# One weight load for two moving blocks in narrow expert bodies, an earlier branch, and a later first wo remainder

## The reference

```python
logits = tokens @ gate_weight.T            # tokens: layer-normed x, 2048 x 512; 8 experts
probs, top1 = softmax(logits), argmax(logits)
mask = one_hot(top1) * (rank_within_expert < 320)   # capacity 320
hmid = gelu(dispatch @ wi)                 # per expert: (<=320) x 512 @ 512 x 2048
eout = hmid @ wo                           # (<=320) x 2048 @ 2048 x 512
out  = combine(probs_of_top1, eout)
x = x + 0.5 * out
```

## Time and profile before

| | us |
|---|---|
| median of 3 runs | 1097.07 |
| lowest and highest | 1093.5, 1099.37 |
| the profiled execution | 1096.42 |
| its span, first to last instruction | 1094.7 |
| TensorE busy in it | 1044.4 (95%) |
| VectorE busy | 721.1 (66%) |
| ScalarE busy | 543.7 (50%) |
| mean granted clock of TensorE, of full speed | 0.977 |

### The profile page before, as it was taken

How to read it: one execution, slowest core, us unless ns; L and a number is a source line. 1 busy time by engine, 2 the same in 40 slices (tenths; PEclk the granted TensorE clock), 3 DMA queues, 4 the chain that set the end, 5 groups by cost and what they waited for, 6 DMA issues and landing times.

```text
span 1094.7 us, 20908 instructions
## 1 busy us (share of the span) xinstructions
PE 1044.4 (95%) x7888; PEld 987.2 (90%) x7888; DVE 721.1 (66%) x1091; ACT 543.7 (50%) x851; POOL 144.3 (13%) x138
## 2 busy tenths in 40 slices
PE   9699999999999999599999996999999999999995
PEld 6699999999999999378777776999999999999995
DVE  8556565776577686477786774557777777665552
ACT  5445455565556565253342324355665656554441
POOL 3201111203021110100000022002212021130101
PEclk9899999999999999899999996999999999999998
DMA  8468546566464761500011244437566575664510
GB/s 309 176 240 303 185 173 215 181 222 206 161 235 156 251 208 38 178 1 1 1 39 39 80 144 147 153 116 244 202 229 213 190 244 185 228 211 142 169 39 25
DMA packets 83276, 177.32 MB, mean 162 GB/s; under 512 B 4192, under 2 KB 4704, under 8 KB 83168
## 3 DMA queue, kind: packets, MB, share of 16 engines
q1 hardware_dynamic: 75488, 152.61, 40.6%
q0 software_dynamic: 7168, 23.07, 6.0%
q10 hardware_dynamic: 576, 1.05, 0.3%
HBM read 162.04 MB, written 18.87 MB: 165 GB/s over the span
## 4 chain that ended last, share of the span: by engine, by line
PE 90%; DVE 4%; DMA 2%; issue 1%; ACT 1%; POOL 1%; POOLq 0%; ACTq 0%; SPq 0%; DVEq 0%
PE psH L1226 13%; PE psH L1227 13%; PE psH L1228 13%; PE acc L1234 12%; PE acc L1235 12%; PE acc L1233 12%; PE acc L1226 3%; PE acc L1228 3%; PE acc L1227 3%; DVE row_stats L831 1%; PE psH L1357 1%; PE psH L1458 1%; DVE dtl L798 1%; PE psT L1286 1%; PE psT L1559 1%
## 5 line engine op out<-in xcount | busy, mean ns | idle before, releaser
L1226 PE MATMUL psH<-dth,wih 128*128 128x240 f32 (+5 forms) x1024 | 295.0, 288 | 0.0
L1234 PE MATMUL acc<-htl,woh 128*128 128x240 f32 (+5 forms) x1024 | 293.4, 287 | 0.0
L1227 PE MATMUL psH<-dtl,wih 128*128 128x240 f32 (+5 forms) x1024 | 293.4, 287 | 0.0
L1235 PE MATMUL acc<-hth,wol 128*128 128x240 f32 (+5 forms) x1024 | 293.2, 286 | 0.0
L1228 PE MATMUL psH<-dth,wil 128*128 128x240 f32 (+5 forms) x1024 | 293.2, 286 | 0.0
L1233 PE MATMUL acc<-hth,woh 128*128 128x240 f32 (+5 forms) x1024 | 293.2, 286 | 0.0
L798 DVE TENSOR_TENSOR wol<-raw_wo,woh 128x1024 fp32r<-128x1024 f32 x128 | 155.7, 1223 | 146.6 <-ACT woh L615 143.5
L649 ACT ACTIVATE gel<-psH 128x320 f32<-128x320 f32 x256 | 111.8, 437 | 189.1 <-PE psH L1228 178.8
L615 ACT ACTIVATE woh<-raw_wo 128x1024 fp32r<-128x1024 f32 x128 | 134.6, 1059 | 132.3 <-PE acc L1235 132.1
L1226 PEld LDWEIGHTS psH<-dth,wih 128*128 128x128 f32 x1024 | 193.1, 189 | 0.4
L1227 PEld LDWEIGHTS psH<-dtl,wih 128*128 128x128 f32 x1024 | 193.0, 188 | 0.0
(11 more groups left out here) (195 smaller groups left out, 1145.4 us busy)
## 6 DMA issues: line engine op xcount, KB each, us to landing
raw_wi<-in_wi SPq DMA_DIRECT2D x64, 1024.0 KB
raw_wo<-in_wo SPq DMA_DIRECT2D x64, 1024.0 KB, 5.4
out_x<-xt SPq DMA_DIRECT2D x4, 1024.0 KB, 5.9
xt<-in_x SPq DMA_DIRECT2D x6, 512.0 KB, 8.2
xt<-x SPq DMA_DIRECT2D x3, 1024.0 KB, 9.7
raw_u<-in_wuT SPq DMA_DIRECT2D x1, 1024.0 KB
raw_u<-in_wvT SPq DMA_DIRECT2D x1, 1024.0 KB
xt<-in_x ACTq DMA_DIRECT2D x2, 256.0 KB, 3.8
```

What stands on the lines that cost most here:

```text
L1226: pe.matmul(out, lh, rh, start=first, stop=False)
L1227: pe.matmul(out, lh, rl, start=False, stop=False)
L1234: pe.matmul(out, lh, rl, start=False, stop=False, skip_group_check=True)
L1235: return pe.matmul(out, ll, rh, start=False, stop=False, skip_group_check=True)
```

## The change

1. *Joined blocks.* `hth` and `htl` become two halves of one tile `ht`. Up to width 256 (`JOINT`), `onto` makes woh·hth and woh·htl one matmul with a moving block of 2 x w columns. It writes hth's part to the lower 256 columns of the bank and htl's to the upper. For wider bodies it stays at three matmuls. ScalarE's copy of the lower part into `eoT` now counts as `eoT_copied`, and VectorE adds `joint` times the upper half (1 for narrow experts, 0 for wide) and counts `eoT_sum`, for which TensorE waits.
2. *Widths.* 192 is new, `WIDTHS` has seven entries. The visited bodies are 288 and 240 in the first layer, all but 272 in the second.
3. *Branch first.* Narrow bodies turn the tokens and the former expert's rows themselves, behind the branch; wide ones turn tokens ahead of the branch and rows behind it.
4. *First wo remainders.* VectorE makes wol of the next expert's step 0 behind the first of the three evictions instead of ahead of the token remainders, and wol of step 1 behind the split of step 0.
5. `clear_acc` writes zeros. The memsets of the banks cover more columns, and GpSimd sets `least` by six memsets.

```diff
-WIDTHS = range(240, CAP + 1, 16)
-NARROW = 2
+WIDTHS = (192, 240, 256, 272, 288, 304, 320)
+NARROW = 3
+JOINT = WIDTHS[NARROW - 1]
-VISITED = (2, 6)
+VISIT = ((288, 240), (192, 240, 256, 288, 304, 320))
-        hth = put("hth", [P, 2, ICS, CAP], F32R)
-        htl = put("htl", [P, 2, ICS, CAP], F32R)
+        ht = put("ht", [P, 2, ICS, 2, CAP], F32R)
+        hth, htl = ht[:, :, :, 0, :], ht[:, :, :, 1, :]
@@ VectorE, expert
-                        wo_split(e, b)
+                        if i > 0:
+                            wo_split(e, b)
                         hidden_split(e, a)
+                        if i == 0:
+                            wo_split(e, b)
...
-                        if not last or a + 2 < STEPS:
+                        if a + 2 < STEPS:
                             wo_split(e, a + 2)
+                    for c in range(DC):
+                        dve.wait_ge(s.acc_done, DC * (PAIRS * e + PAIRS) + c + 1)
+                        dve.wait_ge(s.eoT_copied, DC * e + c + 1)
+                        dve.scalar_tensor_tensor(eoT[:, c, 0:JOINT], acc[c][:, JOINT:], joint_now[:, side:side + 1],
+                                                 eoT[:, c, 0:JOINT], ALU.mult, ALU.add).then_inc(s.eoT_sum, 1)
...
+                        if i == 0 and not last:
+                            wo_split(e + 1, 0)
@@ TensorE
-            def onto(out, lhs, rhs):
-                (lh, ll), (rh, rl) = lhs, rhs
-                pe.matmul(out, lh, rh, start=False, stop=False, skip_group_check=True)
-                pe.matmul(out, lh, rl, start=False, stop=False, skip_group_check=True)
-                return pe.matmul(out, ll, rh, start=False, stop=False, skip_group_check=True)
+            def onto(bank, w, lhs, both):
+                lh, ll = lhs
+                if w <= JOINT:
+                    pe.matmul(bank.rearrange("p (r q) -> p r q", r=2)[:, :, 0:w], lh, both[:, :, 0:w],
+                              start=False, stop=False, skip_group_check=True)
+                else:
+                    for r in range(2):
+                        pe.matmul(bank[:, 0:w], lh, both[:, r, 0:w], start=False, stop=False, skip_group_check=True)
+                return pe.matmul(bank[:, 0:w], ll, both[:, 0, 0:w], start=False, stop=False, skip_group_check=True)
...
                 def expert(e, w, s=s):
+                    if w <= JOINT:
+                        turn_tokens(e, CHUNKS - 1)
+                    turn_out(e)
                     pe.wait_ge(s.dt_lo, DC * e + 3)
```

More of the change, by code:

```diff
@@ L453, in _ @@
                       channel_multiplier=1, allow_small_or_imprecise_dtypes=True).then_inc(pool_const, 1)
[L454 to L455 removed]
+            for k, w in enumerate(WIDTHS[:-1]):
+                ins = pool.memset(least[:, :, k:k + 1], float(w))
+            ins.then_inc(pool_const, 1)
             def power(g, q, var_sem, rstd_sem):
@@ L945, in tables @@
                 then(dve.tensor_copy(dst_now[:, 0, :], dst[:, 0:CHUNKS]))
+                then(dve.tensor_copy(joint_now[:, 0:1], joint[:, 0:1]))
                 settle()
+            dve.memset(nil[:, :], 0.0)
             for bank in acc[:2]:
-                dve.memset(bank[:, 2 * P:CAP], 0.0).then_inc(banks_set, 1)
-            for bank in (*acc[2:], *psH):
+                dve.memset(bank[:, JOINT:], 0.0).then_inc(banks_set, 1)
+            for bank in acc[2:]:
+                dve.memset(bank[:, :], 0.0)
+            for bank in psH:
                 ins = dve.memset(bank[:, 0:CAP], 0.0)
@@ L1436, in mm2 @@
                             d = slice(c * P, (c + 1) * P)
-                            ins = onto(acc[c][:, 0:w], (woh[:, k, j, d], wol[:, k, j, d]),
-                                       (hth[:, k, j, 0:w], htl[:, k, j, 0:w]))
+                            ins = onto(acc[c][:, :], w, (woh[:, k, j, d], wol[:, k, j, d]), ht[:, k, j])
                         if k == 1:
@@ L1501, in _ @@
                     pe.br_lt(width, NARROW, on_true=f"narrow_{n}", on_false=f"wide_{n}")
-                    for what, chunks, ks in (("narrow", CHUNKS - 1, range(NARROW)), ("wide", CHUNKS, range(NARROW, NW))):
-                        with nc.body(f"{what}_{n}", parent=head, valid_engines=[pe.engine]):
-                            pe.wait_ge(s.dn_done, CHUNKS * e + CHUNKS)
-                            for c in range(DC):
-                                if c < 2:
-                                    pe.wait_ge(s.eoT_done, DC * e + c + 1)
-                                turn_tokens(e, c, chunks)
-                            turn_out(e)
-                            dispatch(what, ks)
+                    with nc.body(f"narrow_{n}", parent=head, valid_engines=[pe.engine]):
+                        dispatch("narrow", range(NARROW))
+                    with nc.body(f"wide_{n}", parent=head, valid_engines=[pe.engine]):
+                        turn_tokens(e, CHUNKS)
+                        dispatch("wide", range(NARROW, NW))
                     nc.switch_bb(f"join_{n}", parent=head)
@@ L1519, in _ @@
                         pe.br(f"join_{n}")
-                    if k >= VISITED[n]:
+                    if w not in VISIT[n]:
                         continue
-                    with nc.body(f"visit_{w}_{n}", parent=visits[n][k], valid_engines=[pe.engine]):
+                    with nc.body(f"visit_{w}_{n}", parent=visits[n][VISIT[n].index(w)], valid_engines=[pe.engine]):
                         pe.addr_align(BLOCK, offset=BLOCK - 1, max_nops=0)
```

40 lines of the change are left out of this document (25 added, 15 removed).

## The result

The changed kernel takes 1138.93 us (median of 4 runs, 1136.67 to 1140.64), against 1096.12 for the kernel before in the same session: a ratio of 1.038, 95% interval 1.0353 to 1.0405. Forecast were 1090.3 us and a range up to 1099. The profiled execution took 1138.42 us with a span of 1136.7, 42.0 more than the span before.

The account below looks back on a forecast made before the run. The prediction took experts as bound by TensorE's matmul stream, with TensorE waiting for VectorE between experts. Its sum was 1096.42-13.9+6.0+1.1+0.7 = 1090.3 us, range 1082.5 to 1099.

Parts of the forecast that it names:

- Joined blocks: Second-product matmuls of experts up to 256 wide: two instructions per triple instead of three, first product unchanged at 192; -13.9 us.
- rival 4: VectorE's CAST into the new ht layout takes 0.83 us instead of 0.49, giving 1100.7 us; chance 0.07.
- The remainder of wo: First pair of narrow experts: reordered VectorE work makes TensorE wait 0.53 us (240) or 0.89 (192) for htl; +6.0 us.
- Rival 5: Other pairs at 192: the 0.02 us to spare become waits of 0.1 to 0.3, twelve times; 1091.5 to 1093.9; chance 0.15.
- The sum of halves: Four new VectorE instructions per expert: 0.08 us at each of 14 transitions (+1.1), 0.35 at each layer's end (+0.7).
- Branches, memsets, the rest: Earlier branch in narrow bodies and larger memsets: taken as 0; late bodies at 256, 272, 304 up to 1 us each.
- Rival 6: Bodies of TensorE's program arrive late after a branch, 1 to 5 us in all, giving 1091.3 to 1095.3; chance 0.06.

Follow-up runs that it names:

- g7: g5 with the 240-wide body ahead of the 192-wide one in the program and the lists of branches ahead: 1088.5 us, 0.9941 of the kernel before.
- f1: The kernel before with one list changed: bodies branched to ahead in the first layer are 288 and 240 instead of 240 and 256; 1112.0 us.
- e1: The changed kernel with the turning of tokens and rows put back ahead of the branch, seven bodies kept: 1117.1 us, 1.019 of the kernel before.
- g9: The kernel before with ten more two-column matmuls (repeated clearing of the banks) in each wide body: 1119.3 us, 1.023 of the kernel before.
- g5: The changed kernel with 192 replacing 272 (six bodies, all six visited in layer two), without the earlier branch, first wo remainders in the old order: 1093.6 us.

## Why the prediction was wrong, step by step

**Joined blocks** (-13.9): right in its sum. At 192 the pair takes 0.286 us for a predicted 0.288, at 240 0.327 for 0.3315, and the 192-wide first product stays at 0.112. That the sum at 192 is so close is in part luck: it is made of 0.198 and 0.088, where 0.176 and 0.112 were forecast. Taken from g7's experts, which have the same matmuls and no new wait (40.29 us on average at 192, 42.7 at 240, 45.70 at 256, for 43.27, 43.27 and 46.33 before), the term is -14.8 us. The CAST into the new layout takes 494 ns, so rival 4 is out. The 192-wide expert takes 41.00 us, for a predicted 41.1. Timeline of TensorE in the changed kernel, a 192-wide expert's first pair (start, length):

```profile
876.66 0.25 PE L1261 MATMUL acc<-ht,wol 128*128 128x192 f32 x1
876.75 0.36 PE L1256 MATMUL acc<-ht,woh 128*128 128x384 f32 x1
876.94 0.25 PE L1261 MATMUL acc<-ht,wol 128*128 128x192 f32 x1
877.68 0.44 PE L1256 MATMUL acc<-ht,woh 128*128 128x384 f32 x1 [0.49 <-DVE ht L803]
```

**The remainder of wo** (+6.0): right in its mechanism, somewhat too large. The wait stands where it was put: the matmul at 877.68 starts 0.74 us behind the one ahead, which is otherwise 0.09. The same place in a 240-wide expert has 0.42 for 0.11:

```profile
387.03 0.27 PE L1261 MATMUL acc<-ht,wol 128*128 128x240 f32 x1
387.45 0.49 PE L1256 MATMUL acc<-ht,woh 128*128 128x480 f32 x1 [0.15 <-DVE ht L803]
```

The view of waits gives 2.3 us for it in all, but it counts from the modelled end of the matmul ahead; what it costs is in the experts' times. The changed kernel's 192-wide experts take 41.00 to 41.18 us and its undisturbed 240-wide ones 43.09 to 43.11; in g7, whose VectorE has the old order, they take 40.20 to 40.39 and 42.69 to 42.73. So it is 0.8 and 0.4 us each for a predicted 0.89 and 0.53, 4.6 us in the eight for 5.7; at 256 there is nothing (45.72 and 45.70). A part of the difference is VectorE's order, which ran 0.12 ahead of my list: these rows of VectorE's timeline answer to the earlier trace rows, with the expert's first matmul at 869.34.

```profile
869.56 0.74 DVE L1101 SCALAR_TENSOR_TENSOR rows<-psH,facts_now,rows 64x512 f32<-64x512 f32 x1 [0.42 <-PE psH L1487]
870.23 1.21 DVE L803 TENSOR_TENSOR wol<-raw_wo,woh 128x1024 fp32r<-128x1024 f32 x1
871.36 1.39 DVE L1101 SCALAR_TENSOR_TENSOR rows<-psT,facts_now,rows 128x512 f32<-128x512 f32 x2
...
875.15 1.22 DVE L803 TENSOR_TENSOR wil<-raw_wi,wih 128x1024 fp32r<-128x1024 f32 x1
```

wil starts 5.81 behind the expert's first matmul, not 5.93. The transitions take most of it back in g7 (3.4 us from expert to expert at 192 there, 2.8 in the changed kernel).

In the other pairs one small wait did come, in three of the four 192-wide experts: 33.4 us into the expert a matmul of the first product starts 0.33 to 0.34 us behind the one ahead instead of 0.11, its weight load waiting for ScalarE's gelu. Rival 5 had such waits at twelve places and behind the split.

**The sum of halves** (+1.1, +0.7): right within its bounds, about twice the size taken. Switches that load nothing take 2.81 to 2.84 for 2.66, 0.15 to 0.18 each where 0.08 was taken; the end of the program got 0.3 longer. With these three terms as measured the sum would be some 1089 us, an estimate from the numbers above: the arithmetic of the experts was right, and the whole miss lies in the step that follows.

**Branches, memsets, the rest** (0): this step failed, and with it the result. I took 0 for the earlier branch, because TensorE's queue had no hole behind the branch of before, and "up to 1 us" for a late body of 256, 272 and 304. Rival 6 priced late bodies at 1 to 5 us in all, with a chance of 0.06. Three errors are in this. The row without a hole stood at a switch from 240 to 240, where nothing can be missing. The price of a miss was guessed: it is 2.4 to 4.4 us of standing at a switch (3.4 at 774.77), and a slower clock behind it. And I looked for it at three widths that are not visited, while it came at six of the nine changes of body, at both layers' starts (9.4 and 9.2 us) and in bodies visited ahead. What sets it off, each alone in a run, is a seventh body with its list (29 to 34 us), 243 instructions instead of 223 in the wide bodies (24.5 us) and another list (17.8 us). That all three are one matter of room is my reading.

The profile before held the warning: one instruction packet during the second to eighth expert with five changes of body. That says that a change costs nothing because the next body is held, not because the turning hides it, and the question for a change that adds a body and lengthens the others is how much more can be held. On that the Trainium skill (Runtime: NRT & Kernel Launch, Instruction fetch mechanics) gives 128 KiB for TensorE, filled in blocks of 16 KiB or 256 instructions; an estimate from this page is eight blocks, of which six bodies and the loop's head take seven. The runs fit that only in part: six bodies are free and seven are not, but with another list six load anew as well (f1), and no kernel enters more than five bodies in the first layer and three in the second. So it isn't the bodies in use that must fit, and by which rule a block is given up stays open. The same section says that only two blocks are held, and that a taken branch outside them forces a load before the engine goes on. The stands of 3.4 us agree with the second half of this; the two blocks don't, as the single packet before shows, and the measurement decides.

## What to carry to other kernels

Before adding a specialised copy of a loop body or lengthening one, count the instructions of all of them, and count the packets on the instruction queue in stretches where bodies change: none there means that they are held, and that this is worth protecting. A gain of 2.3 us in each of four experts was buried under 2.6 to 5.5 us at each of six switches and some 9 us at each layer's start. When issue shows up among an engine's waits behind a branch, look at that queue first, and at the engine's own work last.

## What was unexpected of the hardware

- What a matmul costs depends on the one ahead of it: at 192 the joined 384-column matmul takes 0.198 us to the next start and the 192-column one behind it 0.088, below the 0.112 between 192-column matmuls in a row. It looks as if the wider one made room for a part of the next loads; no run separates that.
- Extra instruction packets cost 1.1 to 2.7 us each in the eleven kernels with at least four of them (21.3 us for 19 packets in e1, 24.5 us for 9 in g9, 42.8 us for 25 in the changed kernel; the gains of the experts are in these numbers where a kernel has them). Most of it is TensorE standing, some is the lower clock.
- The order in which bodies stand in the program, with the lists in the same order, is worth as much as an optimisation: 5.1 us between g5 and g7, which differ in nothing else, or 4.2 when each is taken against the kernel before in its own session; 4.1 of it stand at one switch and the expert behind it.
